# Interweaving the split products of two tiles, so that neighbouring matmuls write different PSUM banks

## What is computed

```python
x = x + 0.5 * ffn(layernorm(x))
x = x + attention(layernorm(x))
x = x + 0.5 * ffn(layernorm(x))

# ffn: token shift, then gated squared relu
xr = mu_r * x + (1 - mu_r) * x_prev;  xk = mu_k * x + (1 - mu_k) * x_prev
r = sigmoid(xr @ W_r.T);  k = xk @ W_k.T
out = r * (relu(k)**2 @ W_v.T)

# attention: linear, 16 heads of 16, all tokens of a batch
q = relu(x @ Wq.T)/4;  k = relu(x @ Wk.T)/4;  v = x @ Wv.T;  u = silu(x @ Wu.T)
kv = sum over tokens of k^T v, per head
out = (srms_norm(q @ kv) * u) @ Wo.T
```

## Time and profile before

| | |
|---|---|
| median of three runs | 313.02 us |
| span of the profiled execution | 311.3 us |
| PE matmuls busy | 303.8 us (98%), 2044 instructions |
| PE weight loads busy | 276.2 us (89%), 2044 instructions |
| DVE busy | 240.4 us (77%) |
| ACT busy | 235.3 us (76%) |
| POOL busy | 214.1 us (69%) |
| mean granted TensorE clock | 0.997 |

### The profile page before, as it was taken

The page is one execution under the profiler, slowest core; times in us unless marked ns, Lnnn a source line. Parts: engine busy times, 40 slices in busy tenths (PEclk is TensorE's granted clock), DMA queues, the critical chain, the costliest instruction groups (busy, mean ns, idle before and its releaser), DMA issues.

```text
span 311.3 us, 5822 instructions
## 1 busy us (share of the span) xinstructions
PE 303.8 (98%) x2044; PEld 276.2 (89%) x2044; DVE 240.4 (77%) x586; ACT 235.3 (76%) x461; POOL 214.1 (69%) x236
## 2 busy tenths in 40 slices
PE   6999999999999999999999999999999999999995
PEld 5688889989988988988989998989999999999884
DVE  3989894675756846995894699586979797999695
ACT  2896959779589579679359448669797979699981
POOL 4487977779678687669169314815798979758833
PEclk9999999999999999999999999999999999999998
DMA  7970000000000000000000000000002010101134
GB/s 215 356 241 0 1 3 0 0 2 0 3 0 3 0 0 2 0 2 0 0 3 1 2 0 0 2 1 3 0 3 67 2 67 20 50 2 66 33 106 135
DMA packets 10752, 10.85 MB, mean 35 GB/s; under 512 B 482, under 2 KB 10724, under 8 KB 10724
## 3 DMA queue, kind: packets, MB, share of 16 engines
q1 hardware_dynamic: 10432, 10.23, 10.1%
q10 hardware_dynamic: 292, 0.26, 0.3%
HBM read 6.29 MB, written 4.19 MB: 34 GB/s over the span
## 4 chain that ended last, share of the span: by engine, by line
PE 89%; DVE 6%; ACT 2%; issue 1%; POOL 0%; DVEq 0%; POOLq 0%; ACTq 0%
PE psK L1270 8%; PE psK L1271 8%; PE psK L1272 8%; PE psX L1270 8%; PE psRV L1272 8%; PE psRV L1270 8%; PE psRV L1271 8%; PE psX L1271 7%; PE psX L1272 7%; PE psA L1287 4%; PE psX L1487 2%; PE psK L1474 2%; PE psA L1474 2%; PE psX L1401 2%; PE psRV L1512 1%; PE psRV L1377 1%
## 5 line engine op out<-in xcount | busy, mean ns | idle before, releaser
L939 DVE SCALAR_TENSOR_TENSOR mix<-psA,mu,mix 128x512 f32<-128x512 f32 x60 | 41.5, 744 | 11.6 <-ACT mix L626 11.6
L609 ACT ACTIVATE xn<-xs,shiftA,rstdA 128x256 f32<-128x256 f32 x53 | 27.7, 607 | 15.8 <-POOL shiftA L402 15.8
L418 POOL TENSOR_TENSOR mix_k_lo<-mix,mix_k_hi 128x512 fp32r<-128x512 f32 x26 | 33.3, 1298 | 8.7 <-ACT mix_k_hi L659 8.7
L626 ACT ACTIVATE mix<-psA,one_mu 128x511 f32<-128x511 f32 x60 | 36.9, 698 | 0.6 <-PE psA L1287 0.6
L1270 PE MATMUL psRV<-ffn_hi,mix_r_hi 128*128 128x256 f32 x120 | 34.2, 285 | 0.0
L1272 PE MATMUL psRV<-ffn_hi,mix_r_lo 128*128 128x256 f32 x120 | 33.5, 279 | 0.0
L1271 PE MATMUL psRV<-ffn_lo,mix_r_hi 128*128 128x256 f32 x120 | 33.4, 279 | 0.0
L1270 PE MATMUL psRV<-ffn_hi,act_hi 128*128 128x256 f32 x96 | 27.4, 286 | 0.0
L1272 PE MATMUL psRV<-ffn_hi,act_lo 128*128 128x256 f32 x96 | 26.8, 279 | 0.0
L1271 PE MATMUL psRV<-ffn_lo,act_hi 128*128 128x256 f32 x96 | 26.8, 279 | 0.0
L470 POOL TENSOR_TENSOR k_lo<-k_tok,k_hi 128x512 fp32r<-128x512 f32 x14 | 18.1, 1294 | 11.6 <-ACT k_hi L713 11.6
(11 more groups left out here) (204 smaller groups left out, 1084.0 us busy)
## 6 DMA issues: line engine op xcount, KB each, us to landing
xs<-x_dram SPq DMA_DIRECT2D x7, 512.0 KB, 8.6
out_dram<-xs SPq DMA_DIRECT2D x7, 512.0 KB, 3.0
out_dram<-xs SPq DMA_DIRECT2D x4, 128.0 KB, 1.8
xs<-x_dram ACTq DMA_DIRECT2D x2, 128.0 KB, 3.0
xs<-x_dram SPq DMA_DIRECT2D x2, 128.0 KB, 2.8
silu_u<-w_ffn_k_dram SPq DMA_DIRECT2D x1, 256.0 KB, 4.6
silu_u<-w_ffn_r_dram SPq DMA_DIRECT2D x1, 256.0 KB, 6.3
q_store<-w_k_dram SPq DMA_DIRECT2D x1, 256.0 KB, 6.5
```

What stands on the lines that cost most here:

```text
L418: nc.gpsimd.tensor_tensor(mix_k_lo[:, h, :], mix[:, 0, h, :], mix_k_hi[:, h, :].bitcast(F32), ALU.subtract).then_inc(s_lo_k, 1)
L609: nc.scalar.activation(xn[:, t, :], tile_row(xs, b, t), ACT.Identity, bias=shiftA[:, t:t + 1], scale=rstdA[:, t:t + 1]).then_inc(s_xn, 1)
L626: nc.scalar.activation(mix[:, rk, h, 1:BLOCK], psA[:, h, 0:BLOCK - 1], ACT.Copy, scale=one_mu[:, rk, h:h + 1]).then_inc(s_prev, 1)
L939: nc.vector.scalar_tensor_tensor(out=m, in0=psA[:, h, :], scalar=mu[:, rk, h:h + 1], in1=m, op0=ALU.mult, op1=ALU.add).then_inc(s_mix, 1)
```

## The change

A second helper, `product_of_two`, takes two destinations that share the moving operand and issues their matmuls in turn, so that of two neighbours one writes one bank and one the other. It is used in `ffn_k` (n = 1 to 13), `ffn_r` (n = 1 to 15), `ffn_v` (n = 1 to 11), `k_and_u`, `q_of` and `project_out`. Pairs of tiles are chosen from different banks: tiles t and t + 2 where two tiles share a bank, tiles t and t + 1 in k_and_u, both halves m in ffn_k and q_of. `gram` and `ffn_v` of FFNs 12 to 15 stay as they are. The number of matmuls and weight loads is the same.

The first result of each pair is finished one matmul before the second. Waits move with it: ffn_v waits for both sigmoids before it starts, q_of for both banks of psX; in ffn_k the waits for the second half of the features stand ahead of the seventh matmul.

```diff
+            def product_of_two(first, second, b_hi, b_lo, start, stop):
+                (dst, a_hi, a_lo), (dst2, c_hi, c_lo) = first, second
+                nc.tensor.matmul(dst, a_hi, b_hi, start=start, stop=False)
+                nc.tensor.matmul(dst2, c_hi, b_hi, start=start, stop=False)
+                nc.tensor.matmul(dst, a_hi, b_lo, start=False, stop=False)
+                nc.tensor.matmul(dst2, c_hi, b_lo, start=False, stop=False)
+                return (nc.tensor.matmul(dst, a_lo, b_hi, start=False, stop=stop),
+                        nc.tensor.matmul(dst2, c_lo, b_hi, start=False, stop=stop))
...
 def ffn_k
-                    for m in range(HALVES):
-                        for c in range(HALVES):
-                            part(m, c)
+                    for c in range(HALVES):
+                        pe.wait_ge(s_hi_k, parts(n) + c + 1)
+                        pe.wait_ge(s_lo_k, parts(n) + c + 1)
+                        of = [(psK[:, m, :], ffn_hi[:, 0, c, tok(m)], ffn_lo[:, 0, c, tok(m)]) for m in range(HALVES)]
+                        done = product_of_two(*of, mix_k_hi[:, c, :], mix_k_lo[:, c, :], c == 0, c == HALVES - 1)
+                    for last in done:
+                        last.then_inc(s_k, 1)
...
 def ffn_r
+                if n > 0:
+                    for t in range(2):
+                        for c in range(HALVES):
+                            of = [(psRV[:, g, t * D:(t + 1) * D], mix_r_hi[:, c, tok(2 * g + t)],
+                                   mix_r_lo[:, c, tok(2 * g + t)]) for g in range(2)]
+                            done = product_of_two(*of, ffn_hi[:, 1, c, :], ffn_lo[:, 1, c, :], c == 0, c == HALVES - 1)
+                    for last in done:
+                        last.then_inc(s_r, 1)
+                    return
...
 def ffn_v
+                if 0 < n < SHARED:
+                    pe.wait_ge(s_gate, 2 * n + 2)
+                    for t in range(2):
+                        for c in range(HALVES):
+                            if t == 0:
+                                pe.wait_ge(s_act_lo, lows(n - 1) + c + 1)
+                            of = [(psRV[:, g, t * D:(t + 1) * D], act_hi[:, c, tok(2 * g + t)],
+                                   act_lo[:, c, tok(2 * g + t)]) for g in range(2)]
+                            done = product_of_two(*of, ffn_hi[:, 2, c, :], ffn_lo[:, 2, c, :], c == 0, c == HALVES - 1)
+                    for last in done:
+                        last.then_inc(s_v, 1)
+                    return
...
 def q_of
-                for m in range(HALVES):
-                    pe.wait_ge(s, v - 1 + m)
-                    for c in range(HALVES):
-                        last = product(psX[:, m, :], att_hi[:, c, 2, tok(m)], att_lo[:, c, 2, tok(m)],
-                                       x2_hi[:, c, :], x2_lo[:, c, :], c == 0, c == HALVES - 1)
+                pe.wait_ge(s, v)
+                for c in range(HALVES):
+                    of = [(psX[:, m, :], att_hi[:, c, 2, tok(m)], att_lo[:, c, 2, tok(m)]) for m in range(HALVES)]
+                    done = product_of_two(*of, x2_hi[:, c, :], x2_lo[:, c, :], c == 0, c == HALVES - 1)
+                for last in done:
                     last.then_inc(s_q, 1)
...
 def project_out
-                for t in range(TILES):
-                    dst = psX[:, t // 2, (t % 2) * D:(t % 2 + 1) * D]
+                for t in range(2):
                     for c in range(HALVES):
-                        last = product(dst, g_hi[:, c, tok(t)], g_lo[:, c, tok(t)], wo_hi[:, c, :],
-                                       wo_lo[:, c, :], c == 0, c == HALVES - 1)
-                    if t % 2:
-                        last.then_inc(s_wo, 1)
+                        of = [(psX[:, g, t * D:(t + 1) * D], g_hi[:, c, tok(2 * g + t)], g_lo[:, c, tok(2 * g + t)])
+                              for g in range(2)]
+                        done = product_of_two(*of, wo_hi[:, c, :], wo_lo[:, c, :], c == 0, c == HALVES - 1)
+                for last in done:
+                    last.then_inc(s_wo, 1)
```

## The result

The changed kernel takes 325.0 us in the median of four runs (324.3 to 325.27), the kernel before 313.28 (312.88 to 313.56) beside it: a ratio of 1.0369 [1.0356, 1.0383], slower by 11.7 us. The span of the profiled execution grows from 311.3 to 323.2. All executions in this document had a mean granted TensorE clock of 0.99 or more, except one of e7's four (507 us at 0.561), which is left out of e7's time.

A forecast was written before the change was run, and what follows sets the result against it. PE was taken as the bound (matmuls busy 303.8 of 311.3 us), its pace unchanged; stalls 4.1 + 2.4 + 1.4 + 0.6 + 1.2 + 0.8 = 10.5 give 321.8, plus 1.7 to the median: 323.5 us, range 320 to 327.

The forecast's parts named there:

- Rival (a): All changed products: the bank holds the pace, so they run at fp32's rate, 14.8 us less; 308.7 us, chance 0.12.
- (b): Rival: the products fall into the short pace seen in ffn_r(13), saving 6.5 us; 317.0 us, chance 0.07.
- (e): Rival: the products' pace worsens to gram's 0.120 us a matmul; 326.6 us, chance 0.04.
- (c): Rival: queues give way and only a third to a half of the delays stays; 316 to 319 us, chance 0.08.
- (d): Rival: the delays are absorbed entirely; 313.0 us, chance 0.03.
- three tests: Earlier trace: project_out's and ffn_k(14)'s bank changes and gram(0)'s one-bank fp32 matmuls show no cost for neighbours in one bank.
- Item 1: Second stage: project_out's first half comes 1.14 us later, stalling transpose_g(4) to (7) by 1.07 each; 4.1 us in all.
- Item 2: keep_g (i = 1 to 4): DVE's gate and g_acc come later, so ffn_k and kv wait; 2.4 us in all.
- Item 3: q_of(7), right behind project_out(2), waits for both of its adds; 1.4 us.
- Item 4: k_and_u(6), without transposes ahead of it, waits because ACT's relu chain to x_hi runs 1.0 late; 0.6 us.
- Item 5: Last FFNs: ffn_k(13)'s later first relu delays the tight ACT and DVE chain to transpose_a(15) and ffn_r(14); 1.2 us.
- Item 6: Small waits: project_out(0) and (1) for g_low some 0.2 us each, k_and_u(7) 0.4; 0.8 us, an estimate.

The follow-up runs named there:

- e7: The changed kernel with attend(j+1) ahead of transpose_g(j) in the second stage (n = 8 to 11); 323.2 us, ratio 1.0322 against the kernel before.
- e8: The kernel before plus ten blocks of matmuls behind its end, varying banks, summing, weights, width and fp32; 256-column fp32r took 0.1133 us each in one bank or two.
- e2: The kernel before with only project_out interwoven; 318.44 us, ratio 1.0163.
- e5: The kernel before with only ffn_k (n = 1 to 13) interwoven; 318.59 us, ratio 1.017.
- e4: The kernel before with only ffn_v (n = 1 to 11) interwoven; 316.28 us, ratio 1.0093.
- e6: The kernel before with only ffn_r, k_and_u and q_of interwoven; 317.87 us, ratio 1.0151.
- e3: The change in everything except project_out, which stays as in the kernel before; 322.38 us, ratio 1.0292.
- e10: The kernel before with only ffn_r interwoven; 314.36 us, ratio 1.003.
- e1b: The kernel before, matmul order kept, with the change's waits and each pair's results announced by the last two matmuls; 324.78 us, ratio 1.0371.
- e9: The kernel before plus five blocks of 60 fp32r matmuls behind its end, alone or beside DVE, ACT or POOL work; median step 0.118 us in all.

## Why the prediction was right

The forecast was 323.5, the result 325.0, inside the range and on the forecast's own line of argument.

- **Pace unchanged: right.** project_out(2)'s steps are 0.118; e8 shows it by itself. Rival (a), the bank, is refuted by both; so is (b): in the changed kernel two of 34 runs of 256-column matmuls have the short pace, three of 32 in the kernel before. (e) fails with the 0.118, (c) and (d) with the stalls below, which came in nearly full size. The three tests in the trace of before pointed the right way. I had left open "none of them alternates at every instruction"; e8 does, and it changes nothing. One reading of the earlier trace rows was loose: its 16 are records, two to an instruction, so a plain fp32 instruction takes 0.432; whether a record is itself two passes, as the prediction has it, no run shows.
- **Item 1, transpose_g, 4.1:** measured 0.98, 1.08, 0.96 and 1.07, so 4.1. Right in the place and the size. In e2 the four stalls come from project_out alone, as the working said. In e5 two of them come from ffn_k alone. One detail was wrong: not only the second half, POOL's, is late; PE already waits for DVE's half.
- **Item 2, keep_g, 0.15, 0.72, 0.84, 0.7:** measured 0.13, 0.65, 0.84, 0.74. e4 has them alone (0.13, 0.71, 0.84, 0.80): ffn_v alone is enough, as worked out from the earlier trace rows. It isn't the only function that can stall these places: e6 has 0.31, 0.49 and 0.40 before ffn_k(3), ffn_k(4) and kv(0) without it, e5 0.06, 0.19 and 0.35; beside ffn_v's larger delay they don't show.
- **Item 3, q_of(7), 1.4:** measured 1.42; the stricter wait alone gives 0.94 (e6), the late first add alone 0.83 (e2). **Item 4, k_and_u(6), 0.6:** 0.62, and e5 has it alone, so it is ffn_k's relu.
- **Item 5, the last FFNs, 1.2:** from ffn_k(13) on PE falls back by another 1.1 (10.86 to 11.95 at ffn_r(14)), and ACT's normalize of the earlier trace rows starts at 301.86, 11.96 later than before. Right, with 0.1 less; e5 has the same steps alone (0.42 before ffn_k(14), 0.60 before ffn_r(14)), so it is ffn_k.
- **Item 6, small ones, 0.8:** measured 0.31, 0.31 and 0.49, so 1.1.
- **What was mis-sized:** the span grew by 11.9, the sum says 10.5. 0.53 of the rest lies in the first 7 us, ahead of anything that was changed; that step is 0.53, 0.32, 0.25, 0.02 or -0.20 in other kernels with the same code there, so it is no effect of the change. The six items as measured sum to 10.7, with 0.3 more in item 6 and 0.1 less in item 5. The rest, 0.7, is small steps that I hadn't seen, 1.0 in all: a good half is the extra 0.1 after a wait (six places), 0.37 are short waits inside gram (before q_of(1), q_of(3), attend(0) and project_out(2)), the others are the two paces. 0.31 is given back before project_out(7) and ffn_k(13), where 40 matmuls fell into the short pace, 0.18 of it.
- **Right for the whole, wrong in a part:** the working of item 1 has every engine late by the same amount in every turn. That holds for project_out's delay. For ffn_k's and ffn_r's it is every second turn (e3, e5, e10). In the sum it didn't show, since the larger delay counts alone. That is luck: in e3, with project_out as before, the four turns pay 2.0 and not the 4.1 of that working.
- **ffn_r was put at nothing**, since the later sigmoids "stay behind longer work" and k_and_u lies behind ffn_r. In the second stage there is no k_and_u, and ffn_r alone costs 1.0 us (e10: 0.34, 0.37 and 0.36 in three places). In the changed kernel the larger delays stand before the same transpose_g(4) and (6).
- **ACT's wait for psK** was to grow by 1.1 per block; it grew by 1.03.

The Trainium skill (Perfetto Trace Analysis, Matmuls) asks for groups that rotate through banks so that one is evacuated while the next is computed. e1b shows what giving that up costs here, together with the stricter waits: 11.4 us, with the matmuls in the order of before. The rule holds. The Trainium skill (TensorE: Matmul & The Clock Gate, Back-to-back issue gap) gives N/2.4 + 2.5 ns as the gap of isolated matmuls, 109 ns for 256 columns; no block of fp32r here ran under 113.

## What to carry to other kernels

Interweaving two accumulations didn't speed up either here, and it postpones the first result by nearly a block's length. Before doing it, look who reads that first result: where its queue is closed up until PE needs the outcome, the whole delay ends up on PE, and at several such places of one turn the largest counts, not their sum (transpose_g), unless one wait stands right behind the other (q_of(7)). Look at the waits that move with it too: q_of's wait for both banks cost 0.94 us by itself. Whether a supposed penalty exists at all can be read from start times in the trace, at the places where the old order already changes bank.

## What the runs showed of the hardware

- A 256-column fp32r matmul follows its neighbour after 0.1133 or 0.118 us. One of the two holds for a whole run of matmuls without a hole; a change of bank, of summing or of weights within the run, or work of DVE, ACT or POOL that begins beside it, doesn't change it (e8, e9). What picks it at the start is open. The 512-column ones took 0.227 to 0.228 in e8, 0.229 in k_and_u and 0.233 in ffn_k and q_of.
- Plain fp32 takes 0.216 per record and 0.432 per instruction of 256 columns, nearly four times an fp32r one.
- After a wait the second matmul of a product comes about 0.1 us later than the pace: 0.34 for 0.23 (q_of(7)), 0.20 for 0.118 (project_out(0)). Ahead of a product a stall costs its wait and this.
